# A selective-scan front in another order, and zeros for the sorted rows written during attention

## What is computed

```
xn = layernorm(x)
x  = x + selective_ssm(xn) + moe_8_experts(xn)          # layer 0
xn = layernorm(x)
x  = x + attention_16_heads(xn) + moe_60_experts_top4(xn)  # layer 1

selective_ssm(x):
  dt, B, C = split(x @ x_proj_w.T, [128, 16, 16])
  delta    = softplus(dt @ dt_proj_w.T + dt_proj_b)
  h_t      = exp(delta_t * A) * h_{t-1} + delta_t * B_t * x_t     # 256 channels x 16 states
  y_t      = sum_n(h_t * C_t) + D * x_t
```

## Time and profile before

| what | value |
|---|---|
| runs, us | 1813.85, 1816.66, 1820.73; median 1816.66 |
| the profiled execution, us | 1827.84, span 1826.1 |
| busy, share of the span | PE 93%, DVE 65%, ACT 56%, POOL 43% |
| PE busy, 0 to 98 us | 45.28 of 98, granted clock 0.81 |
| PE busy, 98 to 265 us (scan loop) | 163.79 of 167, granted clock 1.00 |
| PE busy, 341 to 1340 us (attention) | 957.89 of 999, granted clock 0.99 |
| DMA, 341 to 1340 us | 0.06 of the DMA engines' time, 20 GB/s |

### The profile page before, as it was taken

How to read it: one execution, slowest core, us unless ns; L and a number is a source line. 1 busy time by engine, 2 the same in 40 slices (tenths; PEclk the granted TensorE clock), 3 DMA queues, 4 the chain that set the end, 5 groups by cost and what they waited for, 6 DMA issues and landing times. The chain is left out here.

```text
span 1826.1 us, 33417 instructions
## 1 busy us (share of the span) xinstructions
PE 1696.7 (93%) x9234; PEld 1360.4 (74%) x9234; DVE 1194.3 (65%) x2422; ACT 1018.6 (56%) x2287; POOL 778.9 (43%) x789
## 2 busy tenths in 40 slices
PE   6399999489999999999999999999998999999997
PEld 2256556378888888888888888888885777666775
DVE  4799973597887766766767676667662344333476
ACT  4599943267665656665666566666652444434322
POOL 1489861453234544434443444344431342211463
PEclk9699999799999999999999999999999999999999
DMA  4653238500000100000000000001006999999433
GB/s 148 262 221 110 97 116 273 180 12 1 15 9 7 41 13 21 21 6 26 14 11 20 20 20 20 6 26 47 18 30 218 322 325 313 313 302 304 138 95 91
DMA packets 100395, 193.29 MB, mean 106 GB/s; under 512 B 15460, under 2 KB 59748, under 8 KB 97748
## 3 DMA queue, kind: packets, MB, share of 16 engines
q1 hardware_dynamic: 58836, 108.76, 19.1%
q0 software_dynamic: 17152, 47.67, 8.1%
q10 hardware_dynamic: 24336, 35.98, 5.9%
HBM read 140.84 MB, written 51.51 MB: 105 GB/s over the span
## 5 line engine op out<-in xcount | busy, mean ns | idle before, releaser
L1435 POOL TENSOR_TENSOR sw<-sw,rope_t 64x512 f32<-64x512 f32 x128 | 166.1, 1297 | 520.7 <-ACT sw L1048 495.1
L1077 ACT ACTIVATE pb<-ps,negmax 128x128 f32<-128x128 f32 (+7 forms) x256 | 190.8, 745 | 151.2 <-DVE negmax L1288 148.1
L963 PEld LDWEIGHTS ps<-pt,v 128*128 128x128 f32 x1280 | 242.1, 190 | 42.1 <-DVE xr L1316 4.0
L963 PE MATMUL ps<-pt,v 128*128 128x256 f32 (+1 forms) x1280 | 270.7, 358 | 2.8 <-DVE xr L1316 2.6
L561 POOL DMA_DIRECT2D w2r<-in_w x148 | 77.2, 522 | 320.1 <-PE ps L610 278.4
L644 DVE SCALAR_TENSOR_TENSOR ga<-th,ps 128x176 f32<-128x176 f32 x148 | 49.9, 337 | 230.0 <-ACT th L625 230.0
L1288 DVE TENSOR_REDUCE negmax<-ps 128x1 f32<-128x128 f32 (+7 forms) x256 | 193.9, 758 | 8.8
L1064 ACT COPY pt<-ps 128x512 f32<-128x512 f32 (+3 forms) x384 | 171.5, 484 | 38.7 <-PE ps L953 35.6
L1438 POOL TENSOR_TENSOR t<-t,sw 64x512 f32<-64x512 f32 x128 | 167.8, 1311 | 19.2 <-POOL sw L1435 12.8
L593 PE MATMUL ps<-w13r,xt 128*128 128x352 f32 x496 | 169.4, 464 | 0.0
L953 PE MATMUL ps<-ident,pb 128*128 128x128 f32 x1152 | 167.5, 272 | 0.0
(11 more groups left out here) (245 smaller groups left out, 4004.6 us busy)
## 6 DMA issues: line engine op xcount, KB each, us to landing
w13r<-in_w SPq DMA_DIRECT2D x124, 352.0 KB, 5.5
w2r<-in_w POOLq DMA_DIRECT2D x148, 176.0 KB, 5.8
result<-yy ACTq DMA_DIRECT2D x148, 128.0 KB, 4.9
crow<-c_rows SPq DMA_DIRECT2D x32, 512.0 KB, 3.5
t<-sorted SPq DMA_DIRECT2D x124, 128.0 KB, 5.1
sorted<-zeros ACTq DMA_DIRECT2D x15, 1024.0 KB, 16.9
hc<-in_w SPq DMA_DIRECT2D x24, 352.0 KB, 5.1
wraw<-in_wqk SPq DMA_DIRECT2D x16, 256.0 KB
```

The lines of the kernel that those rows point to most:

```text
L963: last = pe.matmul(ps[:, 6, c0:2 * P], v[:, j, hd], pt[g % 2][:, j, c0:2 * P], start=j == 0, stop=j == 2 * g + 1)
L1077: act.activation(pb[:, qt % 2, 0:cols], ps[:, bank:bank + 2, :].rearrange("p a n -> p (a n)")[:, 0:cols], ACT.Exp, bias=negmax[:, par, qn: ...
L1435: g.tensor_tensor(sw[64:128, p % 2, :], sw[64:128, p % 2, :], rope_t[64:128, 1, (p // 2) * 512:(p // 2 + 1) * 512], ALU.mult).then_inc(s_t ...
```

## The change

Three things change. (1) In the front, PE, ACT and DVE are reordered. PE makes the step-size rows of groups 0 and 1 and pieces 0 and 1 first, then B/C rows 0 and 1, step-size rows 2 and 3, pieces 2 and 3, B/C rows 2 and 3, and the routing last. DVE does pieces 0 and 1 first, with the B/C copies between, then routes, then does piece 2, the input rows of batch 0, piece 3 and those of batch 1. (2) ACT's first two decays wait for three and four pieces instead of both for four. (3) Layer 1's zero fill leaves ACT's queue; SP issues it in the attention, as 31 DMAs of 512 rows (512 KB) from a new tile `zero_tile` of 128 x 1024, which DVE fills with zeros before the attention; it stands behind the loads for the second pair of heads and ahead of those for the third. The waits of DVE and ACT for its end go; POOL's stays.

```diff
+        R1.zero_dmas = R1.routed * P // 512
...
+        zero_tile = sbo("zero_tile", [P, 4 * D])
...
# SP, attention: load_pair(hp) is the old body of the loop
-            with sp.Fori(0, PAIRS_H - 1) as hp:
+            load_pair(0)
+            sp.wait_ge(s_kept, 1)
+            for k in range(R1.zero_dmas):
+                sp.dma_start(R1.slots[k * 512:(k + 1) * 512, :].rearrange("(p a) d -> p (a d)", p=P), zero_tile[:]).then_inc(R1.zeroed, 16)
+            with sp.Fori(1, PAIRS_H - 1) as hp:
+                load_pair(hp)
...
# DVE, front: softplus(p), take_bc_rows(q), input_rows(b) hold the old code
+            def softplus(p, between=lambda: None):
...
+                for k in range(4):
+                    if k == 3:
+                        between()
...
+            softplus(0)
+            take_bc_rows(0)
+            take_bc_rows(1)
+
+            def last_bc_rows():
+                take_bc_rows(2)
+                take_bc_rows(3)
+            softplus(1, last_bc_rows)
             v.wait_ge(R0.logits_ready, 1)
...
             route_dve(v, R0)
-
             v.tensor_tensor(R0.weight[:, :, 0], R0.top[:, :, 1], R0.top[:, :, 0], ALU.subtract).then_inc(s_w0, 1)
-            for p in range(BATCH * DC):
...
+            softplus(2)
+            input_rows(0)
+            softplus(3)
+            input_rows(1)
...
# DVE, before the attention
-            v.wait_ge(R1.zeroed, 16 * R1.zero_dmas)
+            v.memset(zero_tile[:], 0.0).then_inc(s_kept, 1)
...
# ACT
-            zero_fill(act, R1)
+            take_group(0)
+            take_group(1)
+            take_dt_rows(0)
+            take_group(2)
+            take_dt_rows(1)
+            take_group(3)
+            act.wait_ge(s_const, N_CONST + 4)
+            softplus(0)
+            take_dt_rows(2)
+            take_dt_rows(3)
+            for p in range(1, BATCH * DC):
+                softplus(p)
...
-                    if isinstance(it, int) and it == 0:
-                        act.wait_ge(s_delta, BATCH * DC)
+                    if isinstance(it, int) and it < 2:
+                        act.wait_ge(s_delta, 3 + it)
...
-            act.wait_ge(R1.zeroed, 16 * R1.zero_dmas)
...
# PE
             def dt_piece(p):
                 b, c = p // DC, p % DC
+                pe.wait_ge(s_xdc, 2 * b + 2)
                 if p >= 2:
                     pe.wait_ge(s_dpc, 2 * p - 2)
+                else:
+                    pe.wait_ge(s_xnT, p + 3)
...
+            turn_group(1)
+            pe.wait_ge(s_par, 80)
+            dt_rows(0)
+            turn_group(2)
+            dt_rows(1)
+            turn_group(3)
+            for p in range(2):
+                dt_piece(p)
+            bc_rows(0)
+            bc_rows(1)
+            dt_rows(2)
+            dt_rows(3)
+            for p in range(2, BATCH * DC):
+                dt_piece(p)
+            bc_rows(2)
+            bc_rows(3)
+            pe.wait_ge(s_bcc, NG)
...
+            route_pe(pe, R0)
             pe.wait_ge(R0.slots_ready, 1)
             delta_rows(0)
             delta_rows(1)
```

More of the change, by code:

```diff
@@ L1803, in _, with take_group, take_dt_rows, softplus @@
             act.mul(aneg[:], alog[:], -1.0).then_inc(s_aneg, 1)
[L1805 to L1815 removed]
+            def take_group(q):
+                act.wait_ge(s_xnT_ps, q + 1)
+                for c in range(DC):
+                    last = act.copy(xnT[:, c, q * 512:(q + 1) * 512], ps[:, (q % 2) * 2 + c, :])
+                last.then_inc(s_xnT, 1)
+            def take_dt_rows(g):
+                act.wait_ge(s_xd, g + 1)
+                act.copy(dtT[:, g * 512:(g + 1) * 512], ps[:, 4 + g % 2, :]).then_inc(s_xdc, 1)
+            def softplus(p):
                 c = p % DC
@@ new lines, in turn_group, with dt_rows @@
+            def turn_group(q):
+                pe.wait_ge(s_xn, q + 1)
+                if q >= 2:
+                    pe.wait_ge(s_xnT, q - 1)
+                for c in range(DC):
+                    for i in range(GT):
+                        last = pe.transpose(ps[:, (q % 2) * 2 + c, i * P:(i + 1) * P], xn[:, q * GT + i, c * P:(c + 1) * P], ident[:])
+                last.then_inc(s_xnT_ps, 1)
+            def dt_rows(g):
+                pe.wait_ge(s_xnT, g + 1)
+                if g >= 2:
+                    pe.wait_ge(s_xdc, g - 1)
+                for c in range(DC):
+                    last = pe.matmul(ps[:, 4 + g % 2, :], xpw[:, c, 0:RANK], xnT[:, c, g * 512:(g + 1) * 512],
+                                     start=c == 0, stop=c == DC - 1)
+                last.then_inc(s_xd, 1)
@@ L1914, in dt_piece, with bc_rows @@
+            def bc_rows(g):
+                pe.wait_ge(s_xnT, g + 1)
+                if g >= 2:
+                    pe.wait_ge(s_bcc, g - 1)
+                for c in range(DC):
+                    last = pe.matmul(ps[0:BCR, 6 + g % 2, :], xpw[:, c, RANK:XD], xnT[:, c, g * 512:(g + 1) * 512],
+                                     start=c == 0, stop=c == DC - 1)
+                last.then_inc(s_xb, 1)
             def dt_piece(p):
                 b, c = p // DC, p % DC
+                pe.wait_ge(s_xdc, 2 * b + 2)
@@ L1920, in dt_piece @@
                               start=True, stop=True).then_inc(s_dp, 1)
-            pe.wait_ge(s_xdc, NG)
-            for p in range(2):
-                dt_piece(p)
-            pe.wait_ge(s_bcc, NG)
-            for i in range(NT):
-                last = pe.transpose(ps[:, 4 + i // 8, (i % 8) * BCR:(i % 8 + 1) * BCR], bcT[:, i * P:(i + 1) * P], ident[0:BCR, 0:BCR])
-            last.then_inc(R0.logits_ready, 1)
-            route_pe(pe, R0)
-            for p in range(2, BATCH * DC):
-                dt_piece(p)
             def delta_rows(b):
@@ L1943, in delta_rows @@
                     last.then_inc(s_dlT, 1)
+            turn_group(0)
+            turn_group(1)
[15 more added lines that the diff above has]
+            pe.wait_ge(s_bcc, NG)
+            for i in range(NT):
+                last = pe.transpose(ps[:, 4 + i // 8, (i % 8) * BCR:(i % 8 + 1) * BCR], bcT[:, i * P:(i + 1) * P], ident[0:BCR, 0:BCR])
+            last.then_inc(R0.logits_ready, 1)
+            route_pe(pe, R0)
             pe.wait_ge(R0.slots_ready, 1)
```

68 lines of the change are left out of this document (16 added, 52 removed).

## The result

| what | before | after |
|---|---|---|
| median of 10 runs each, same chip, us | 1817.60 (1813.85 to 1822.07) | 1804.12 (1798.48 to 1810.23) |
| ratio after / before, 95% interval | | 0.9921 (0.9902 to 0.9941) |
| the profiled execution, us | 1827.84, span 1826.1 | 1798.48, span 1796.8 |
| first scan (DVE) / first spread (PE) | 90.43 / 88.39 | 79.07 / 77.02 |
| PE's first hc sum, from where PE bounds the scan loop | 98.97 | 87.02 |

The change is faster by 0.8% (0.6 to 1.0). By the ratio it gains 14.4 us (10.7 to 17.8), forecast were 12.6.

The account below looks back on a forecast made before the run. PE was taken to bound the scan loop from 98 us on, so its earlier entry counts: 6.0 + 5.4 + 0.6 + 0.6 = 12.6 us off the median 1816.66 gives 1804.0; own range 1799 to 1808, up to 1813 with rivals.

Parts of the forecast that it names:

- PE and ACT up to the second softplus: Front: ACT's first piece starts at 24.1, the next three run back to back from 33.8 until 55.6.
- DVE: Front: with softplus and routing reordered, DVE's last dxT ends at 76.8 against 82.85, 6.0 us earlier.
- Last dxT to first scan: Front: the gap shrinks from 7.6 to 2.2 us because ACT's scaled blocks are ready early, gaining 5.4 us.
- The start of the loop: Scan loop: PE's third state starts 0.6 us sooner, and POOL's wait for a C row goes, another 0.6 us.
- the second 0.6: Scan loop: POOL's wait for a C row during the zero fill, which cost PE 0.6 us, disappears.
- POOL's scatters: Front: sixteen scatters run from 56.2 until 79.5, hidden by 1.8 us before the first product hc.
- The rival of a blocked POOL queue: Front: scatters beside DVE's pieces 2 and 3 slow down, hc comes late, 9.2 us lost, 1813; chance 0.10.
- The clock of PE: Front rival: PE stays at 1.2 GHz from 22 us on, up to 11 us later, gain 1.6, 1815; chance 0.10.
- The zero fill: Attention: SP's 31 DMAs take 41 us, 508.8 to 550, 28 us before POOL's scatter; cost 0, up to +2.
- Cost 0, up to +2 for what this trace doesn't show (transfers and code fetches beside the fill): Attention: moving the zeros to SP's queue costs nothing, at most 2 us, and cannot gain.
- that begins 12 us earlier and ends less than that earlier: Sign of a wrong forecast: a loop starts 12 us sooner but ends with less of that gain.
- The late zeros: Attention rival: DMAs don't overlap, fill lasts 108 us until 617, POOL and PE wait, +27, 1843; chance 0.06.

Follow-up runs that it names:

- e3: Changed kernel plus 16 small ACT copies behind its last softplus piece, in the place of the sixteen DMA issues; ratio to the kernel before 0.9926.
- e10: Changed kernel plus 8 small ACT copies later in the program, in ACT's idle time ahead of the attention; ratio to the kernel before 0.9926.
- e8: Changed kernel run once more without any edit, on another chip; ratio to the kernel before 0.9928.
- e9: Changed kernel plus 16 small ACT copies later in the program, in ACT's idle time ahead of the attention; ratio to the kernel before 0.9913.
- e4: Changed kernel plus 31 more DMAs of zeros to an array nobody reads, ahead of the real ones, POOL waiting for both; ratio to the kernel before 1.0004.
- the padded versions: Changed kernel with 16 or 8 added small ACT copies and no other edit (e3, e9, e10); ratios to the kernel before 0.9926, 0.9913, 0.9926.
- e7: Kernel before plus 112 small ACT copies in its idle time ahead of the attention; ratio to the kernel before 1.0028.
- e1: Changed kernel with the zero fill back on ACT's queue and the old waits for its end, so the new front alone; ratio to the kernel before 0.9931.

## Why the prediction was right

The time, 1804.0 forecast and 1804.12 measured, agrees better than its parts do. By its own steps:

- **PE and ACT up to the second softplus.** Forecast: pieces at 24.1, 33.8, 41.1, 48.3, end 55.6. Measured: 25.01, 34.33, 41.61, 48.85, end 56.2. Each half to one us late, all from the first; DVE's piece 1 ended 0.3 us late.
- **DVE.** Piece 1 until 45.8 (46.1), routing until 55.9 (56.0), dxT of batch 0 until 65.7 (65.9), dxT of batch 1 until 76.8 (76.9). The term of 6.0 us was 82.85 - 76.9 = 5.9.
- **Last dxT to first scan.** 5.4 forecast; 7.6 - 2.2 = 5.4 measured (76.9 to 79.07). The 2.2 holds for a first spread at the 1.2 GHz level, which it had in both profiles; in e3, at 2.4 GHz, it was 1.3.
- **The start of the loop.** 0.6 + 0.6 forecast. The first sum came 98.97 - 87.02 = 11.95 us sooner, the first scan 11.36: 0.6. POOL waited for no C row. The last sum of the scan loop started at 249.5 instead of 262.7, 13.2 us sooner, so the second 0.6 was in truth 1.2 (0.9 of it before the tenth sum), and the entry, 13.25 us sooner, adds nothing. In the other versions with the whole change the entry was 8.0 (e10) to 13.4 us (e3) sooner. Two sources are seen: PE's clock at the start of the loop (last sum at 251.6 in e8, e9 and e10, where the window from 82 to 90 us has 0.50), and PE's waits for sorted rows in layer 0's experts (2.8 us after, 3.6 in e8, 5.4 in e10).
- **POOL's scatters.** End 79.5 forecast, 78.2 measured; slack 3.3 us instead of 1.8. One of them took 2.06 us and one 1.54, the rest 0.96 to 1.02, beside DVE's softplus pieces 2 and 3 and its dxT. The rival of a blocked POOL queue did not come, and the figure of the Trainium skill that stood beside it (SBUF — State Buffer, "A bandwidth-pool intuition that's wrong (but worth ruling out)", 3.1 us) was seen in none of the sixteen. That section gives it for a DVE tensor_copy; here DVE ran scalar_tensor_tensor and tensor_tensor beside the scatters.
- **The clock of PE.** Granted 0.83 from 0 to 98 us, 0.81 before, and 1.00 from 20 to 40 us, where the rival had put 0.50. But the rival was set up for the wrong stretch. From 50 to 80 us the clock stood at 0.50, with PE busy for 2.4 of the first ten microseconds (it had been for 3.3 of the ten before) and for 6.85 of the last ten, which are no longer the nearly idle ones of the earlier trace rows. Here it was back at 1.00 when the loop's second state began; in e8, the same kernel, it was not until 90 us, and the last sum began 2.1 us later, 1.7 of them arisen behind the first scan. So the clock costs nothing against the forecast in the profile that was compared, and up to 2 us in others.
- **The zero fill.** Forecast 41 us from 508.8 to 550, less the 12 by which all is earlier; measured 44 us with the last landing, from 496.60 to 540.5, which is over the 40 that the forecast had named as a sign of being right, and cost nothing. The slack to POOL's scatter was 25 us, forecast 28; e4 shows that it was real and where it ends. The load of head 4's weights was issued at 535.17 behind the zeros and nobody waited for it.
- **"Cost 0, up to +2 for what this trace doesn't show (transfers and code fetches beside the fill)".** This is the step that failed. Nothing beside the fill cost anything, but the sixteen issues that left ACT's program moved its loop across a border of instruction fetches, and 1.1 us a pass, 4.6 to 5.6 us in all, went between entry and exit. The forecast named a loop "that begins 12 us earlier and ends less than that earlier" as a sign of error, and that is what the marks show: 13.25 at the entry, 7.6 at the exit. The total came out all the same. What makes up for these 5 us isn't shown: the ratio's interval, 10.7 to 17.8 us, holds 12.6 but not the 7.6 at the exit, so at least 3 us of the gain arose behind it, where nothing was forecast (if the one profile's 7.6 stands for all executions), and the padded versions gain no more than the unpadded. The forecast was right by its front, which is shown step by step; that the total agrees as well is luck, and the 0.1 us all the more: the medians themselves differ by 13.5 us, of which 12.6 were forecast, and the kernel before was 0.9 us slower in the ten runs than in the three that the forecast started from.

Of the rivals, none came as described. The late zeros could have: the forecast put the point from which they decide at 69 us of fill, and e4, whose zeros let POOL go 83.4 us after the first issue (496.40 to 579.79), puts it at 83.4 - 14.15 = 69.2; the whole gain is gone with it (1.0004).

## What to carry to other kernels

In a chain of two engines, order the steps so that the engine behind gets its first input as early as the one ahead can make it, and put work that nobody waits for (here routing, which feeds only a queue) where the second engine would be waiting; read the gain from the two timelines, step by step. A bulk write belongs where its deadline is far away, and on a queue whose engine computes nothing; here it cost nothing up to the deadline and nearly one for one behind it, so give the distance in us with it. Where the engine that bounds the next stage has little to do for tens of microseconds, read its clock at the start of that stage in more than one execution. After any edit that changes how many instructions an engine runs ahead of a long loop, look for "issue" waits at the same place of each pass and at the instruction queue's packets; a few harmless instructions ahead of the loop tell whether its place is the cause.

## What the runs showed of the hardware that was not expected

- ACT's loop of some 270 instructions costs, or doesn't, by its place alone. With sixteen instructions fewer ahead of it ACT fetched it anew in every pass: 26 instead of 5 to 7 packets of 8 KB in five passes, and on each of the four returns two holes of 2.1 to 2.3 and 1.3 us in ACT, 1.23 us of idle on PE (read in one pass), 1.1 us a pass. It was made to come (e7) and to go (e3, e9, e10). The Trainium skill, Runtime: NRT & Kernel Launch, section "Instruction fetch mechanics", says that a taken branch whose target is outside the window of the current two pages forces a fetch before execution can go on. The traces agree in kind: the holes come on each return to the loop's start, if it starts at the wrong place; the packets here hold 8 KB. How much of its program the engine keeps wasn't measured.
- A queue of ACT's holds the engine: twelve 1 MB DMAs held it for 17.2 us when issued from 67.96, and for 19.3 when issued from 55.88 (e1). The bytes of all sixteen as 31 DMAs of 512 KB on SP's queue went out at 400 to 410 GB/s and took 38.2 us of SP alone. With a queue already full the issuing goes as fast as the bytes drain: e4's second 31 took 40.04 us, 16.25 MB at 406 GB/s.
- The same kernel's scan loop starts at either level of PE's clock: 8 transposes took 1.06 us in the changed kernel from 86.12 and 1.94 in e8 from 86.55, and the second sum came 2.59 us behind the first in one and 3.47 in the other.
